# A four-layer graph network on one core: full-array products in the record scatter, and an accumulator added by an identity product

## The chip, the cores and the metric

The kernel runs on one core of one Trainium2 chip. A core has five engines that run beside each other: TensorE (matrix products; its weight loads are a row of their own in the profile, PEld), VectorE (DVE), ScalarE (ACT), GpSimd (POOL) and SyncE (SP, which here only issues transfers). The metric is the device time of one execution in microseconds (us). The kernel is one program; its stages follow each other with a barrier between them.

## The reference, cut to what matters

A graph of N = 3125 nodes with 256 features and E = 103125 edges (src, dst). Four layers follow each other, each on a normalised x:

```python
h = relu(layernorm(x)); x = x + L0(h, edges, edge_attr_18)     # attention, 16 heads, segments by src
h = relu(layernorm(x)); x = x + L1(h, edges, edge_attr_64, w)  # edge attention, 8 heads, by dst, and a feed-forward
h = relu(layernorm(x)); x = x + L2(h, edges, edge_type_8)      # relation sums, batch norm
h = relu(layernorm(x)); x = x + L3(h, edges)                   # attention, 4 heads, by dst
```

The attention of L1, which one part of the change touches, is, with `s` the scores of an edge per head:

```python
s   = (q[dst] * (k[src] + ef @ We + be)).sum(-1) * scale * edge_weight
ex  = exp(s - segment_max(s, dst)[dst])
out = segment_sum(ex / segment_sum(ex, dst)[dst] * v[src], dst) @ Wo + bo
```

## The kernel before, in words

**Sorting.** The edges are first put in order of their segment, once by src and once by dst. A node number is split into a high part (its block of BN = 126 nodes, NB = 25 blocks) and a low part (its place in the block). Edges come in tiles of 128, eight tiles (G) to a step, 101 steps. `scatter` (L497) runs once per order. Per step:
- VectorE (`position_ones`, L336) compares the keys with a row of numbers and writes one-hots: `hot_hi` (128 edges x 25 per tile) and `hot_lo` (128 x 128), in bf16.
- TensorE turns the high one-hots (L642) and ScalarE copies the result to `hot_hi_t` (25 x 128 per tile, f32, L564). L654 spreads the keys over rows, for the rank within a tile (VectorE, L608).
- A table of 25 x 128 counts says where the next edge of each node goes. L670 adds a pair of tiles to it in PSUM; ScalarE copies it to `table` (L577), two buffers in turn. L675 looks up: `hot_hi_t` of a tile is the stationary operand, the table the moving one, f32, contracting over the 25 high values. Each f32 product is two instructions. VectorE picks the low column (L616) and adds the rank: the position (L625).
- GpSimd writes each tile's records to DRAM with one indirect DMA (L545), eight per step, and waits for the positions, for the attributes that SP loads and for words that ScalarE copies (L588).

Beside the first scatter the high and low counts of the second order are summed (L717). Beside the second one, the q, k and v rows of the first layer are computed: once in four steps TensorE does one full-size f32 product (L845).

**The edge layer.** `edge_layer` (L956) runs for the kinds 0, 1 and 3, each 107 steps of eight tiles. The four engines work on different steps at once; `lagging` gives the step before (older), two before (oldest) and three before (gone). Per step, in kind 1:
- SP loads the records; GpSimd gathers 128 rows of k and v per tile with an indirect DMA (L1120) into one of four buffers, which is free once the sums of four steps ago are done.
- TensorE, in this order: the rest of the expansion of q to edges (L1190), the turned scores (L1204), the sums of the oldest step's first two pairs of tiles (L1230), more expansion, spread low keys (L1142), the turned exponentials (L1217, L1218), the sums of the last two pairs, and the preparation of the step after next.
- VectorE: the edge part is added to k (L1499, half a step at a time), multiplied with q (L1509), reduced to scores (L1532), scaled by the edge's weight (L1538); two scans find the maxima of the segments (L1444, L1448); the oldest step's v is weighed with the exponentials (L1476).
- ScalarE: the one-hots that place edges in rows (L1302, L1311, L1330, L1335), the exponentials (L1340), and `move_sums`, which copies each pair's sums from PSUM to `pair_sums` (L1357).
- A pair of tiles lies in one block of nodes. Its sums (128 x 272) are added to that block's slice of the accumulator `acc` by VectorE (`add_sums`, L1465), four adds per step, a step after the copy. The block's number is loaded to a register (`blocks_of`). The last two rows of `pair_sums` (segments that go on in the next tile) go to DRAM (L1360).

The order on each engine is the order of the calls in its `body`, and semaphores join them; nothing is reordered.

## Time and profile before

| | us |
|---|---|
| median of 3 runs | 8586.36 (8586.0 to 8587.62) |
| the profiled execution | 8571.41 |
| its span, first to last instruction | 8569.7 |
| TensorE busy | 6613.0 (77%) |
| VectorE busy | 5308.7 (62%) |
| GpSimd busy | 5221.6 (61%) |
| ScalarE busy | 3576.5 (42%) |
| mean granted TensorE clock | 0.784 of 2.4 GHz |

The busy shares are means over stages with different limits, so each stage is read by itself. The first scatter issues its DMAs from 285.0 to 1331.6 us, the second from 1359.6 to 2393.4; the layer of kind 0 follows, and that of kind 1 gathers from 4041.8 to 5413.8. Busy times of TensorE are modelled at their ends and overlap a little; for a group of products the distance from its start to the next group's start says more than the durations. Instructions that only issue or wait are not counted as busy. A granted clock of 0.50 is 1.2 GHz, 1.00 is 2.4 GHz.

### The profile page before, as it was taken

The page shows a single profiled execution, that of the slowest core. Times are in us where ns is not written, and L with a number is a line of the kernel's source. Part 1 is how long each engine was busy: PE and PEld are TensorE (multiplying, and loading weights), DVE is VectorE, ACT ScalarE, POOL GpSimd, SP SyncE. Part 2 cuts the span into 40 slices and gives each one's busy share as a digit, 9 for nine tenths or more (in the row PEclk, how much of TensorE's full clock was granted, in tenths as well). Part 3 has the DMA queues.
Part 4 walks back from the last instruction along what each step waited for, and adds up shares of the span by engine and source line. Part 5 has one row for each costly group of instructions (what it writes and reads, how often), then busy time and mean ns, then how long its engine had stood idle before and what let it go on. Part 6 is the DMA issues. An engine that isn't in the chain of part 4 may idle for free. (4 is left out here: it accounts for less than half of the span.)

```text
span 8569.7 us, 143502 instructions
## 1 busy us (share of the span) xinstructions
PE 6613.0 (77%) x33110; PEld 4732.5 (55%) x33111; DVE 5308.7 (62%) x15263; ACT 3576.5 (42%) x10766; POOL 5221.6 (61%) x5120
## 2 busy tenths in 40 slices
PE   7999998999979989974777777667855555667675
PEld 6777775666646666652555555455433344445454
DVE  6677776666657777774999999721122223455556
ACT  3322222333347666632666666223200000777772
POOL 0477776777767777721777777200277775677772
PEclk9655555555589999997999999879877777887887
DMA  7411111111145555532666666200344443444442
GB/s 219 136 17 16 17 17 26 33 33 34 33 106 140 138 136 138 140 61 96 184 175 175 176 178 175 85 11 33 132 108 108 108 108 80 107 110 109 109 108 47
DMA packets 1013468, 849.20 MB, mean 99 GB/s; under 512 B 751678, under 2 KB 841581, under 8 KB 1009339
## 3 DMA queue, kind: packets, MB, share of 16 engines
q0 software_dynamic: 257152, 645.64, 27.7%
q1 hardware_dynamic: 710069, 154.62, 9.1%
q10 hardware_dynamic: 45780, 44.08, 1.5%
q14 instruction: 341, 2.79, 0.1%
q8 instruction: 126, 2.06, 0.1%
HBM read 723.28 MB, written 120.67 MB: 98 GB/s over the span
## 5 line engine op out<-in xcount | busy, mean ns | idle before, releaser
L1120 POOL DMA_INDIRECT edges_kv<-kv,edges_rec x1712 | 1998.4, 1167 | 968.0 <-issue 511.0
L1230 PE MATMUL banks<-edges_kv,edges_hot 128*128 128x288 f32 (+2 forms) x5136 | 1563.8, 455 | 623.3 <-DVE edges_kv L1476 412.9
L1230 PEld LDWEIGHTS banks<-edges_kv,edges_hot 128*128 128x128 f32 x5136 | 1051.9, 215 | 1005.0 <-issue 563.6
L1631 POOL DMA_INDIRECT edges_rows<-rel,edges_rec x856 | 809.3, 945 | 965.2 <-DMA edges_rec<-by_dst_records 710.0
L545 POOL DMA_INDIRECT by_src_records<-sort_by_src_rec,sort_pos_i x808 | 773.9, 958 | 544.2 <-issue 533.2
L1120 POOL DMA_INDIRECT edges_kv<-feat,edges_rec x856 | 829.3, 969 | 270.4 <-issue 253.9
L675 PE MATMUL banks<-sort_table,sort_hot_hi_t 25*128 25x128 f32 x3232 | 952.1, 444 | 52.0 <-DVE sort_junk L616 47.2
L1647 PE MATMUL banks<-edges_rows,edges_hot 128*128 128x256 f32 x1712 | 625.8, 529 | 466.1 <-DMA edges_rows<-rel,edges_rec 449.2
L545 POOL DMA_INDIRECT by_dst_records<-sort_by_dst_rec,sort_pos_i x808 | 773.7, 958 | 288.0 <-issue 250.3
L1465 DVE TENSOR_TENSOR acc<-edges_pair_sums,acc 128x288 f32 (+2 forms) x1284 | 560.6, 437 | 487.0 <-DMA edges_kv<-feat,edges_rec 268.7
L675 PEld LDWEIGHTS banks<-sort_table,sort_hot_hi_t 25*128 25x128 f32 x3232 | 721.5, 307 | 221.2 <-issue 121.1
L1647 PEld LDWEIGHTS banks<-edges_rows,edges_hot 128*128 128x128 f32 x1712 | 428.0, 262 | 664.3 <-issue 404.0
L616 DVE SCALAR_TENSOR_TENSOR sort_junk<-banks,sort_hot_lo 128x128 bf16<-128x128 f32 x1616 | 435.3, 287 | 578.0 <-PE banks L675 537.5
L1330 ACT ACTIVATE edges_off<-columns,edges_column 128x128 bf16<-128x128 f32 x2568 | 784.6, 390 | 0.0
L1679 DVE TENSOR_TENSOR agg<-banks,agg 128x256 f32 x428 | 181.7, 424 | 768.8 <-PE banks L1647 768.8
L1302 ACT ACTIVATE edges_apart<-banks,minus_p 128x512 bf16<-128x512 f32 x642 | 429.3, 686 | 435.0 <-PE banks L1142 226.8
L608 DVE SCALAR_TENSOR_TENSOR sort_junk<-banks,sort_key_cur,sort_earlier 128x128 bf16<-128x128 f32 x1616 | 575.6, 411 | 6.0 <-PE banks L654 6.0
L1357 ACT COPY edges_pair_sums<-banks 128x288 f32<-128x288 f32 (+2 forms) x1284 | 460.7, 383 | 275.6 <-PE banks L1230 246.8
L1476 DVE TENSOR_TENSOR edges_kv<-edges_kv 128x1024 f32<-128x1024 f32 x428 | 518.8, 1212 | 0.0
L577 ACT COPY sort_table<-banks 25x128 f32<-25x128 f32 x808 | 204.8, 254 | 728.2 <-PE banks L670 728.2
L564 ACT COPY sort_hot_hi_t<-banks 25x512 f32<-25x512 f32 x404 | 231.9, 574 | 647.2 <-PE banks L642 647.2
L1190 PE MATMUL banks<-x,edges_hot_t 128*128 x1712 | 476.5, 403 | 3.4 <-DVE edges_kv L1509 3.4
(372 smaller groups left out, 12506.6 us busy)
## 6 DMA issues: line engine op xcount, KB each, us to landing
edges_kv<-kv,edges_rec POOLq DMA_INDIRECT x1712
sort_feat<-in_edge_attr_dram SPq DMA_DIRECT2D x100, 256.0 KB, 3.6
rel<-tables_stage SPq DMA_DIRECT2D x25, 1008.0 KB
by_dst_records<-by_dst_blank ACTq DMA_DIRECT2D x1, 17120.0 KB, 54.2
edges_rec<-by_dst_records SPq DMA_DIRECT2D x107, 160.0 KB
edges_rows<-rel,edges_rec POOLq DMA_INDIRECT x856
edges_kv<-feat,edges_rec POOLq DMA_INDIRECT x856
by_src_records<-sort_by_src_rec,sort_pos_i POOLq DMA_INDIRECT x808, 2.1
```

Of the source, the lines that this page charges most:

```text
L545: pool.indirect_dma_start(O.rec, bass.IndirectOffsetOnAxis(ap=pos_i[:, u, c:c + 1], axis=0), rec[:, u, c, :], None).then_inc(scattered[u], 16)
L608: last = dve.scalar_tensor_tensor(out=junk[:, 0, c, 0:P + mates].rearrange("p (t e) -> p t e", e=P), in0=ps[:, 4 + h, end - P - mates:end] ...
L675: pe.matmul(ps[:, 2 + c % 2, 0:P], hot_hi_t[:, u, c, :], table[:, d % 2, :], start=True, stop=True).then_inc(looked_up, 1)
L1120: pool.indirect_dma_start(kv[:, r, c, 0:koff + DIM], None, tab, bass.IndirectOffsetOnAxis(ap=reci[:, r, c, idx:idx + 1], axis=0)).then_inc ...
L1190: last = pe.matmul(out[:, c, 2 * P - QW:2 * P], hot_t[:, b % 2, 2 * m + c, :], rows, start=(kind == 1), stop=(kind == 1 or c == 1), skip_g ...
L1230: last = pe.matmul(ps[:, 6 + m % 2, 0:OW], hot[:, b % 2, c, :], kv[:, b % BUFS, c, koff:koff + OW], start=(c % 2 == 0), stop=(c % 2 == 1))
L1330: last = act.activation(off[:, c, :], C.columns[:, c % 2, :], ACT.Abs, bias=column[:, b % 2, c:c + 1], scale=-1.0)
L1357: act.copy(pair_sums[:, m, :], ps[:, 6 + m % 2, 0:OW]).then_inc(sums_copied, 1)
L1465: dve.tensor_tensor(rows, pair_sums[:, m, :], rows, ALU.add).then_inc(added, 1)
L1476: dve.tensor_tensor(v4, v4, bc(exps, dh), ALU.mult).then_inc(msg_done, 1)
L1631: pool.indirect_dma_start(rows[:, b, c, :], None, tab, bass.IndirectOffsetOnAxis(ap=reci[:, b, c, idx:idx + 1], axis=0)).then_inc(gathered ...
L1647: last = pe.matmul(ps[:, m, 0:DIM], hot[:, b, c, :], rows[:, b, c, :], start=(c % 2 == 0), stop=(c % 2 == 1))
```

## The change

In `scatter`, the tiles that feed three products are made 128 high or wide, with zeros in what was not there; the zeros are written once, by GpSimd, at the start. The products L642, L670 and L675 run over all of it. In the edge layer of kind 1, VectorE's adds go; TensorE adds the accumulator's block to the pair's sums in PSUM by a product with the identity, and ScalarE copies the sum back to the accumulator, and the 32 rows from 96 on to `pair_sums`. Each such product waits until the accumulator of the pair before it has been stored. ScalarE's third pair moves into `one_hot`, between the two passes of the one-hots.

```diff
-        hot_hi = ph.sbuf("hot_hi", [P, 2, G, NB], BF16)
+        hot_hi = ph.sbuf("hot_hi", [P, 2, G, P], BF16)
-        hot_hi_t = ph.sbuf("hot_hi_t", [NB, 2, G, P])
+        hot_hi_t = ph.sbuf("hot_hi_t", [P, 2, G, P])
-        table = ph.sbuf("table", [NB, 2, P])
+        table = ph.sbuf("table", [P, 2, P])
...
+                pool.memset(table[:], 0.0).then_inc(filled, 1)
+                pool.memset(hot_hi_t[:], 0.0).then_inc(filled, 1)
+                pool.memset(hot_hi[:], 0.0).then_inc(filled, 1)
...
-                            last = pe.matmul(ps[0:NB, 0, P * c:P * c + P], hot_hi[:, b % 2, 4 * h + c, :], C.ident_b[:],
+                            last = pe.matmul(ps[:, 0, P * c:P * c + P], hot_hi[:, b % 2, 4 * h + c, :], C.ident_b[:],
...
-                                last = pe.matmul(ps[0:NB, TABLE, 0:P], hot_hi[:, u, c, :], hot_lo[:, u, c, :],
+                                last = pe.matmul(ps[:, TABLE, 0:P], hot_hi[:, u, c, :], hot_lo[:, u, c, :],
...
                         for c in (2 * m, 2 * m + 1):
                             last = pe.matmul(ps[:, 6 + m % 2, 0:OW], hot[:, b % 2, c, :], kv[:, b % BUFS, c, koff:koff + OW],
-                                             start=(c % 2 == 0), stop=(c % 2 == 1))
-                        last.then_inc(summed, 1)
+                                             start=(c % 2 == 0), stop=(kind != 1 and c % 2 == 1))
+                        if kind != 1:
+                            last.then_inc(summed, 1)
+
+                def with_past(j, b, m):
+
+                    n = at(j, b)
+                    block = blocks_of(pe, O, j, b, UNROLL)[m]
+                    if not (first_steps(j, b, 1) and m == 0):
+                        pe.wait_ge(acc_kept, n(PAIRS, m))
+                    pe.matmul(ps[:, 6 + m % 2, 0:OW], C.ident[0:BN, :],
+                              acc[0:BN, bass.ds(block, 1), :].rearrange("p o w -> p (o w)"), start=False, stop=True).then_inc(summed, 1)
...
                     if oldest:
                         sums(*oldest, 0)
+                        if kind == 1:
+                            with_past(*oldest, 0)
                     if inside:
                         expand(j, b, (3,))
+                    if oldest and kind == 1:
+                        with_past(*oldest, 1)
...
                     if oldest:
                         sums(*oldest, 1)
+                        if kind == 1:
+                            with_past(*oldest, 2)
                     if ahead:
                         expand(*ahead, (1,))
                     if beyond:
                         front(*beyond)
+                    if oldest and kind == 1:
+                        with_past(*oldest, 3)
...
-                def move_sums(j, b, h):
+                def move_sums(j, b, pairs):
...
+                    blocks = blocks_of(act, O, j, b, UNROLL) if kind == 1 else None
+                    for m in pairs:
                         act.wait_ge(summed, n(PAIRS, m + 1))
+                        if kind == 1:
+                            act.copy(acc[:, bass.ds(blocks[m], 1), :].rearrange("p o w -> p (o w)"), ps[:, 6 + m % 2, 0:OW]
+                                     ).then_inc(acc_kept, 1)
+                            act.copy(pair_sums[ENDS:P, m, :], ps[ENDS:P, 6 + m % 2, 0:OW]).then_inc(sums_copied, 1)
+                            continue
...
+                    if between:
+                        move_sums(*between, (2,))
...
                     older, oldest, gone = (lagging(j, b, lag) for lag in (1, 2, 3))
+                    if kind == 1:
+                        gone = None
```

`ENDS` is 96. Not shown: the slices `0:NB` where the 25 rows or columns are written, and `move_sums` being called for the pairs (0, 1), (2) and (3) instead of two halves.

## Rows read from the trace of the kernel before

**Rows 1.** Windows, first and second scatter: stretch, length, busy (count) by engine, granted clock, DMA, GB/s.
```profile
285.10:1331.70 1046.60, 973.00 (x5582) 729.90 (x5581) 769.70 (x3699) 272.37 (x1192) 772.93 (x808) 0.50 0.16 28
1359.70:2393.40 1033.70, 939.44 (x4918) 647.05 (x4918) 668.68 (x3660) 312.51 (x1464) 772.68 (x808) 0.54 0.16 33
```

**Rows 2.** Line L545: count, ns min/median/max, first and last start.
```profile
L545 POOL DMA_INDIRECT by_src_records<-sort_by_src_rec,sort_pos_i x808: 952/958/1177, 285.0 to 1331.6; - x162
L545 POOL DMA_INDIRECT by_dst_records<-sort_by_dst_rec,sort_pos_i x808: 952/958/973, 1359.6 to 2393.4; - x162
```

**Rows 3.** Order of time, first scatter: start, us, engine, line, [idle before].
```profile
1001.71 0.96 POOL L545 DMA_INDIRECT by_src_records<-sort_by_src_rec,sort_pos_i  x1 [0.30 <-issue]
...
1002.16 0.12 PEld L670 LDWEIGHTS banks<-sort_hot_lo,sort_hot_hi 128*25 128x25 bf16 x2 [0.23 <-issue]
...
1006.65 0.11 PEld L654 LDWEIGHTS banks<-sort_ident_hi,sort_halves 128*128 128x128 bf16 x1 [0.20 <-issue]
```

**Rows 4.** Line L1532: count, ns min/median/max, first and last start.
```profile
L1532 DVE TENSOR_REDUCE edges_score_raw<-edges_kv x107: 2268/2270/2286, 4058.9 to 5422.2; 128x64 f32<-128x2048 f32 x107
```

**Rows 5.** Window of the edge layer of kind 1.
```profile
4058.97:5422.25 1363.28, 1030.06 (x4733) 761.82 (x4731) 1269.79 (x2110) 853.78 (x2318) 1051.76 (x844) 0.94 0.64 176
```

**Rows 6.** Order of time in kind 1: VectorE, and one GpSimd issue.
```profile
4804.78 2.27 DVE L1532 TENSOR_REDUCE edges_score_raw<-edges_kv 128x64 f32<-128x2048 f32 x1
...
4807.46 1.21 DVE L1499 TENSOR_TENSOR edges_kv<-edges_kv,edges_rec 128x1024 f32<-128x1024 f32 x1
4808.59 0.43 DVE L1465 TENSOR_TENSOR acc<-edges_pair_sums,acc 128x272 f32 x1
4808.95 1.27 DVE L1509 TENSOR_TENSOR edges_kv<-banks,edges_kv 128x512 f32<-128x512 f32 x2
4810.15 1.21 DVE L1476 TENSOR_TENSOR edges_kv<-edges_kv 128x1024 f32<-128x1024 f32 x1
4811.28 0.43 DVE L1465 TENSOR_TENSOR acc<-edges_pair_sums,acc 128x272 f32 x1
...
4812.93 1.21 DVE L1499 TENSOR_TENSOR edges_kv<-edges_kv,edges_rec 128x1024 f32<-128x1024 f32 x1
...
4816.75 2.27 DVE L1532 TENSOR_REDUCE edges_score_raw<-edges_kv 128x64 f32<-128x2048 f32 x1
...
4810.15 2.38 POOL L1120 DMA_INDIRECT edges_kv<-kv,edges_rec  x1 [0.31 <-issue]
```

**Rows 7.** By line, same stretch: count, busy us, mean ns, idle before and its releasers.
```profile
L1120 POOL DMA_INDIRECT edges_kv<-kv,edges_rec x844 | 1052.0, 1246 | 304.4 <-issue 242.8 <-PE banks L1230 61.6
...
L1499 DVE TENSOR_TENSOR edges_kv<-edges_kv,edges_rec 128x1024 f32<-128x1024 f32 x212 | 257.5, 1215 | 59.7 <-DMA edges_kv<-kv,edges_rec 38.9 <-issue 20.6
...
L1465 DVE TENSOR_TENSOR acc<-edges_pair_sums,acc 128x272 f32 x415 | 177.7, 428 | 0.0
L1357 ACT COPY edges_pair_sums<-banks 128x272 f32<-128x272 f32 x418 | 148.4, 380 | 64.2 <-PE banks L1230 56.1
```

**Rows 8.** Order of time, second scatter, TensorE.
```profile
1534.35 1.22 PE L675 MATMUL banks<-sort_table,sort_hot_hi_t 25*128 25x128 f32 x4
...
1536.86 3.72 PE L845 MATMUL banks<-sort_qkv_w,sort_cur_t 128*128 128x512 f32 x4
...
1542.45 0.71 PE L675 MATMUL banks<-sort_table,sort_hot_hi_t 25*128 25x128 f32 x4
```

**Rows 9.** Order of time, the start of the kernel.
```profile
13.26 0.64 POOL L274 MEMSET sort_by_dst_rec<- 128x640 f32 x1
...
54.92 1.76 SPq L407 DMA_DIRECT2D sort_feat<-in_edge_attr_dram  x4
```

**Rows 10.** Order of time in kind 1: TensorE, and ScalarE.
```profile
4811.45 2.07 PE L1230 MATMUL banks<-edges_kv,edges_hot 128*128 128x272 f32 x8 [1.82 <-issue]
4813.36 1.03 PE L1190 MATMUL banks<-x,edges_hot_t 128*128 x4
...
4804.40 2.45 ACT L1330 ACTIVATE edges_off<-columns,edges_column 128x128 bf16<-128x128 f32 x8
```

More of the change, by code:

```diff
@@ L552, in _ @@
                 def _(act):
-                    act.copy(table[:, 0, :], starts[:]).then_inc(table_ready, 1)
+                    act.copy(table[0:NB, 0, :], starts[:]).then_inc(table_ready, 1)
                     beside.scalar_start(act)
@@ L563, in turn @@
                         act.wait_ge(turned, at(j, b)(2, h + 1))
-                        act.copy(hot_hi_t[:, b % 2, 4 * h:4 * h + 4, :], ps[0:NB, 0, :].rearrange("k (c e) -> k c e", c=4)
+                        act.copy(hot_hi_t[0:NB, b % 2, 4 * h:4 * h + 4, :], ps[0:NB, 0, :].rearrange("k (c e) -> k c e", c=4)
                                  ).then_inc(turned_copied, 1)
@@ L576, in body @@
                             act.wait_ge(looked_up, n(G, 2 * d))
-                            act.copy(table[:, (d + 1) % 2, :], ps[0:NB, TABLE, 0:P]).then_inc(table_ready, 1)
+                            act.copy(table[0:NB, (d + 1) % 2, :], ps[0:NB, TABLE, 0:P]).then_inc(table_ready, 1)
                             if ahead and d == 0:
@@ L631, in _ @@
                 def _(pe):
-                    pe.matmul(ps[0:NB, TABLE, 0:P], C.zeros_b[:, 0:NB], C.zeros_b[:], start=True, stop=False, skip_group_check=True)
+                    pe.matmul(ps[:, TABLE, 0:P], C.zeros_b[:], C.zeros_b[:], start=True, stop=False, skip_group_check=True)
                     pe.matmul(ps[0:NB, TABLE, 0:P], C.ident[0:NB, 0:NB], starts[:], start=False, stop=False, skip_group_check=True)
@@ L972, in edge_layer @@
     UNROLL = 12
+    ENDS = 96
     ROUNDS = -(-STEPS // UNROLL)
@@ L1081, in edge_layer @@
         added = ph.sem("added")
+        acc_kept = ph.sem("acc_kept")
         dve_set = ph.sem("dve_set")
@@ L1324, in front, with one_hot @@
                     last.then_inc(front_copied, 1)
-                def one_hot(j, b):
+                def one_hot(j, b, between=None):
                     n = at(j, b)
@@ L1346, in tails @@
                              ps[:, 0, 2 * P:2 * P + 2 * HG].rearrange("p (i c h) -> p i c h", i=2, c=G)).then_inc(tail_copied, 1)
-                def move_sums(j, b, h):
+                def move_sums(j, b, pairs):
                     n = at(j, b)
-                    if h == 0:
+                    if 0 in pairs:
                         act.wait_ge(ends_out, n(16, 0))
-                    for m in (2 * h, 2 * h + 1):
+                    blocks = blocks_of(act, O, j, b, UNROLL) if kind == 1 else None
+                    for m in pairs:
                         act.wait_ge(summed, n(PAIRS, m + 1))
+                        if kind == 1:
[3 more added lines that the diff above has]
+                            continue
                         if not first_steps(j, b, 1):
@@ L1357, in move_sums @@
                         act.copy(pair_sums[:, m, :], ps[:, 6 + m % 2, 0:OW]).then_inc(sums_copied, 1)
-                    if h == 1:
+                    if PAIRS - 1 in pairs:
                         act.wait_ge(sums_copied, n(PAIRS, PAIRS))
@@ L1385, in body @@
                     if oldest:
-                        move_sums(*oldest, 0)
+                        move_sums(*oldest, (0, 1))
                     if ahead and kind < 3:
@@ L1394, in body @@
                     if older:
-                        one_hot(*older)
+                        one_hot(*older, oldest if kind == 1 else None)
+                    elif oldest and kind == 1:
+                        move_sums(*oldest, (2,))
                     if older and kind == 3:
@@ L1398, in body @@
                     if oldest:
-                        move_sums(*oldest, 1)
+                        move_sums(*oldest, (3,) if kind == 1 else (2, 3))
                 steps(act, body)
```

2 lines of the change are left out of this document (1 added, 1 removed).

## The prediction

> **What bounds the kernel now.** I read the busy shares by slice first and kept the two stretches that the change touches: the scatter of sorted records (L497 to L683, run twice) and the edge layer of kind 1 (L956 to L1578). Then the windows of each, then the work grouped by line, then the order of work in single steps.
>
> The scatters look bound by TensorE: it is busy 973.00 of 1046.60 us and 939.44 of 1033.70 us, at a granted clock of 0.50 and 0.54 of 2.4 GHz [rows 1]. They are not. GpSimd issues 808 indirect DMAs in each; from first to last start it needs (1331.6 - 285.0) / 807 = 1.297 us per DMA in the first and (2393.4 - 1359.6) / 807 = 1.281 in the second [rows 2], and a DMA with nothing to wait for costs 0.96 + 0.30 = 1.26 us [rows 3]. So 98% of each scatter is GpSimd's own issue time, and TensorE sits just under it.
>
> The edge layer has 107 steps. The last reduction starts at 5422.2, the first at 4058.9 [rows 4]: 1363.3 / 106 = 12.86 us per step. VectorE is busy 1269.79 of 1363.28 us [rows 5], and a step without a disturbance takes 4816.75 - 4804.78 = 11.97 us [rows 6], in which VectorE never rests. GpSimd: (1052.0 busy + 242.8 issue gap) / 844 x 8 = 12.27 us per step, and 61.6 / 844 x 8 = 0.58 us more in which it waits for L1230 to free a buffer [rows 7]: 12.85 together, the whole step. VectorE in turn waited 59.7 us before L1499, mostly for gathers [rows 7]. So two engines share the bound: GpSimd's issue (12.27), VectorE (11.97), and 0.59 us lost because neither is steady.
>
> **The change, part by part: the scatter.** Removed: nothing. L642, L670 and L675 keep their number and their moving columns; the high one-hot is 128 columns wide as a stationary operand where it was 25, and L675 contracts over 128 rows where it was 25. Each first weight load took 0.12 us at 25 columns and 0.11 us at 128 [rows 3], so at the same clock the cost is nil; bounds from the 0.01 us either way, on 6 first loads a step and 202 steps: -12 to +12 us of TensorE, which lies beside GpSimd.
>
> Can the clock change? In the second scatter the one full-array f32 product, L845, runs 3.72 us; L675 before it costs 1.22 us a group and after it 0.71 us [rows 8]. The same L675 with its 25 rows ran 93% of the first scatter [rows 1] and never left 1.2 GHz. So full-array work is what preceded the rise, and the change makes three more products full-array. I expect a higher clock in both scatters.
>
> The Trainium skill, "TensorE: Matmul & The Clock Gate", section "Part 1: The HAM clock gate", says that a busy TensorE releases the throttle. The trace speaks against it as it stands: 93% busy and throttled. By the page's rule, which knows only busy or idle, the change would lift nothing.
>
> What is a higher clock worth? Little. The first scatter loses 0.016 us per DMA against the second, 807 x 0.016 = 13 us, and both together lose 807 x (0.037 + 0.021) = 47 us against the bare 1.26. Not all of that is TensorE's: the second scatter has its clock raised in part already, and both wait for records and code. I take 10 us, nearest to the 13 by which the two differ. Bounds: 0 and 47. Next to be late is GpSimd itself, which nothing here makes faster.
>
> Three more memsets on GpSimd (256 f32, 2048 f32 and 2048 bf16 per partition): 640 f32 took 0.64 us, so about 4.4 us behind the memsets at 13.3 us. This block ends with SP's loads; SP's first DMA of the next one starts at 54.92 [rows 9]; they are hidden, and would cost their 4.4 us without that cover.
>
> **The edge layer of kind 1.** Removed: four L1465 adds per step on VectorE. Each fills 4808.95 - 4808.59 = 0.36 us of its line (0.428 by its own duration, less the overlap) [rows 6, 7]: about 4 x 0.35 = 1.40 us. One of them covers the time between the reduction and the product that waits for it; I give back 0.1. VectorE: 11.97 - 1.40 + 0.1 = 10.7 us.
>
> Added on TensorE: four f32 products per step, 126 rows, 272 moving columns, each two instructions. The eight instructions of L1230 take 4813.36 - 4811.45 = 1.91 us [rows 10], so one product 0.48 us and four 1.9. TensorE was busy (1030.06 / 1363.28) x 12.86 = 9.7 us a step [rows 5] and becomes 11.6.
>
> Added on ScalarE: four more copies, by the 0.380 us of L1357 [rows 7] 1.5 us on an engine that is busy 853.78 of 1363.28, or 8.1 us a step [rows 5]: 9.6, no bound.
>
> Moved, and the new waits: product m waits until ScalarE has stored the accumulator of product m-1. Behind the waiting product stand L1190 and the transposes, for which VectorE waits. Of the four waits, m=0 is long fulfilled. Between m=0 and m=1 lie the expansion L1190 (1.03 us), longer than one copy of 0.38: covered. m=2 is old. m=3 waits for a copy that ScalarE makes after its eight L1330 (2.45 us) [rows 10]; behind it are the next expansion and the transpose of the scores. The first product alone costs VectorE something: L1230 starts at 4811.45, L1190 ends at 4813.36 + 1.03 = 4814.39 [rows 10], and becomes 4814.87. VectorE wants that bank after the scan block (4812.93 - 4811.28 - 0.35 = 1.30), L1499 (4808.59 - 4807.46 = 1.13) and half of the two L1509 (0.60): 4811.28 + 3.03 = 4814.31 [rows 6]. It waits 0.56: 11.25 us. TensorE's own 11.6 includes overlaps and slow-clock time, so I take 11.5 for the ring of VectorE, TensorE and ScalarE; its bounds are 10.7 (every wait covered) and 11.6 + 4 x (0.38 + 0.1) = 13.5 (no copy covered).
>
> GpSimd. Its mean issue is 1.246 us in this stage against 0.95 undisturbed. The one that starts at 4810.15 takes 2.38 us and ends at 4812.53, 0.90 us after the slot of L1465 (4811.28 + 0.35 = 4811.63) [rows 6]. So an issue that begins under L1476 and L1465 starts anew when they end; under the reduction L1532 none does. The stretching costs 12.27 - 8 x 1.25 = 2.3 us per step. The ops that do it fill 2 x 1.13 (L1499), 2 x 1.13 (L1476) and 1.40 (L1465) us: by time L1465's share is 24%; by the square of each unbroken stretch (three of 1.49, one of 1.13 and one of 0.34 become four of 1.13) it is 37%. I take 30%, 0.7 us: GpSimd 11.6 us per step; bounds 0 (another op merely takes the place) and 0.85.
>
> The Trainium skill, "SBUF — State Buffer", section "SBUF: two separate sides", says that a VectorE instruction with two SBUF inputs shuts out a GpSimd operation that reads SBUF until it ends. L1465, L1476 and L1499 have two SBUF inputs, L1509 and L1532 have not, and the trace agrees with the 2.38 us.
>
> The sum. The slower of 11.5 and 11.6, and the same 0.59 lost to unsteadiness: 12.2 us. (12.86 - 12.2) x 106 = 70 us. The profiled execution takes 8571.41 us, 8569.7 of it the span; 8571.4 - 10 - 70 = 8491. The median of the runs, 8586.36, lies 15.0 above the profiled time: **8506 us**.
>
> **The rivals.**
> - Steadier than before: with 1.27 us less VectorE work the engines stop disturbing each other, and a step falls to about 11.5. 1.36 x 106 = 144 us, with the scatter 154: 8432. For it: the gathers that came late did so behind long issues. Against it: after a late gather TensorE drops to 1.2 GHz (mean 0.94 here [rows 5]), and it now has 1.9 us more to catch up with.
> - GpSimd isn't relieved: its 12.27 stays, with half of the 0.59: 12.56, 32 us, 10 from the scatter: 8544; with none of either 8586. For it: issues fall by turns on one op or another.
> - Slower: the ring closes through ScalarE. In the in-order queue of TensorE the product m=3 waits behind L1330, the next step's scores wait behind it, and VectorE's scan behind them. At the 13.5 bound a step costs 0.64 more: +68, less 10: 8644. It decides from the point where the ring exceeds 12.86, that is where 1.4 us of the copies and of the register loads ahead of each product lie open. For it: every step at 1.2 GHz doubles TensorE's 1.9. Against it: two of the four waits are covered by a microsecond.
> - The widening doesn't lift the clock: then the scatter gives 0: 8516.
> - The scatters are TensorE-bound after all: at full clock some 40% of the 973 + 939 us would go, 760 us. The 1.26 of [rows 3] excludes nearly all of it.
>
> **How the numbers follow.** Forecast 0.45; same with the clock not lifted 0.15; steadier 0.14; GpSimd unrelieved 0.12; slower 0.11; TensorE-bound scatters 0.03. Likeliest case alone: 8465 to 8550. Range for 8 in 10: 8430 to 8590, from the steadier case to no change at all. This kernel's runs tell apart 0.2%, 17 us. Faster: 0.45 + 0.15 + 0.14 + 0.03, plus half of the unrelieved case, less 0.04 for shortfalls within 17 us: 0.79. Same 0.09, slower 0.12.
>
> **What would show it.** Right: clock near 1 in the scatters with L675 near 0.7 us a group, yet 1.26 to 1.28 us per DMA of L545; L1532 starting every 11.3 to 11.6 us when undisturbed and 12.2 on average; L1120 in this layer near 1.16 us; L1465 gone there. Wrong: scatters shorter by over 47 us; L1120 still at 1.24; VectorE waiting over 1 us per step before L1444 or L1509 for TensorE.

## The result, and the profile after

The changed kernel takes 8542.28 us, the median of 5 runs (8530.89 to 8547.64); the kernel before took 8586.0 (8579.67 to 8587.62) beside it. The ratio is 0.995, with a 95% interval of 0.9936 to 0.9965: faster, by 44 us. The forecast was 8506 in a range of 8430 to 8590. So direction and range held, but the gain is about half of the 80 us forecast.

The profiled execution took 8530.89 us, its span 8529.2, against 8571.41 and 8569.7. First the windows of the two scatters (columns as in [rows 1]) and the scattering line (as in [rows 2]) of the changed kernel:

```profile
280.00:1313.90 1033.90, 698.13 (x5577) 607.05 (x5577) 758.60 (x3699) 272.55 (x1190) 772.90 (x808) 0.75 0.17 29
1339.20:2368.00 1028.80, 691.42 (x4918) 577.36 (x4918) 653.16 (x3662) 313.10 (x1464) 772.70 (x807) 0.75 0.16 33
```

```profile
L548 POOL DMA_INDIRECT by_src_records<-sort_by_src_rec,sort_pos_i x808: 954/958/1177, 279.9 to 1313.9; - x162
L548 POOL DMA_INDIRECT by_dst_records<-sort_by_dst_rec,sort_pos_i x808: 952/958/975, 1339.2 to 2368.0; - x162
```

The granted clock rose from 0.50 and 0.54 to 0.75, and TensorE's busy time fell by 275 and 248 us. Yet a scatter needs 1034.0 / 807 = 1.281 and 1028.8 / 807 = 1.275 us per DMA, against 1.297 and 1.281: 12.6 and 5.0 us won.

Then the edge layer of kind 1: its window, its last reduction, and the work by line, to be read against [rows 4, 5, 7]:

```profile
4033.20:5363.00 1329.80, 1202.11 (x5568) 880.42 (x5566) 1164.29 (x1695) 1016.58 (x2729) 902.82 (x843) 0.98 0.66 181
```

```profile
L1565 DVE TENSOR_REDUCE edges_score_raw<-edges_kv x107: 2272/2279/2289, 4033.2 to 5362.9; 128x64 f32<-128x2048 f32 x107
```

```profile
L1125 POOL DMA_INDIRECT edges_kv<-kv,edges_rec x843 | 903.1, 1071 | 417.0 <-issue 272.1 <-PE banks L1246 144.9
...
L1532 DVE TENSOR_TENSOR edges_kv<-edges_kv,edges_rec 128x1024 f32<-128x1024 f32 x212 | 260.0, 1227 | 66.3 <-DMA edges_kv<-kv,edges_rec 43.0 <-issue 22.6
...
L1542 DVE TENSOR_TENSOR edges_kv<-banks,edges_kv 128x512 f32<-128x512 f32 x424 | 276.9, 687 | 33.5 <-PE banks L1195 11.0
...
L1477 DVE TENSOR_TENSOR_SCAN edges_run_max<-edges_pen,banks 64x128 f32<-64x128 f32 x106 | 43.5, 410 | 60.9 <-PE banks L1209 60.5
...
L1246 PE MATMUL banks<-acc,ident 126*128 x836 | 281.0, 417 | 48.6 <-ACT acc L1382 38.3 <-issue 5.1
...
L1382 ACT COPY acc<-banks 128x272 f32 x418 | 158.9, 380 | 170.4 <-PE banks L1246 162.7 <-DMA ends<-edges_pair_sums 4.0 <-issue 0.6
```

From first to last reduction 1329.7 us, 12.54 a step, against 1363.3 and 12.86. VectorE is 105 us less busy. A gather issue takes 1.071 us in place of 1.246 [rows 7]. But GpSimd now waits 144.9 us for L1246, where it waited 61.6 for L1230, and VectorE waits 60.5 us for L1209 before its scan, where it waited for nothing. The order of time shows where that wait and VectorE's new one come from, in one step without a disturbance (TensorE, ScalarE, GpSimd, VectorE in turn):

```profile
4362.81 2.00 PE L1235 MATMUL banks<-edges_kv,edges_hot 128*128 128x272 f32 x8
4364.64 0.62 PE L1246 MATMUL banks<-acc,ident 126*128 x2
...
4367.08 0.72 PE L1246 MATMUL banks<-acc,ident 126*128 x2 [0.37 <-ACT acc L1382]
4367.97 1.12 PE L1195 MATMUL banks<-x,edges_hot_t 128*128 x4 [0.17 <-issue]
4368.93 0.27 PE L1209 MATMUL banks<-ident,edges_score 128*64 128x128 f32 x1
...
4364.00 2.44 ACT L1353 ACTIVATE edges_off<-columns,edges_column 128x128 bf16<-128x128 f32 x8
4366.35 0.36 ACT L1382 COPY acc<-banks 128x272 f32 x1
...
4363.51 0.94 POOL L1125 DMA_INDIRECT edges_kv<-kv,edges_rec  x1 [0.30 <-issue]
...
4368.61 0.94 POOL L1125 DMA_INDIRECT edges_kv<-kv,edges_rec  x1 [1.66 <-PE banks L1246]
...
4371.17 1.41 POOL L1125 DMA_INDIRECT edges_kv<-kv,edges_rec  x1 [0.30 <-issue]
...
4362.30 2.28 DVE L1565 TENSOR_REDUCE edges_score_raw<-edges_kv 128x64 f32<-128x2048 f32 x1
...
4364.75 1.25 DVE L1532 TENSOR_TENSOR edges_kv<-edges_kv,edges_rec 128x1024 f32<-128x1024 f32 x1
4366.13 1.29 DVE L1542 TENSOR_TENSOR edges_kv<-banks,edges_kv 128x512 f32<-128x512 f32 x2
...
4369.24 0.41 DVE L1477 TENSOR_TENSOR_SCAN edges_run_max<-edges_pen,banks 64x128 f32<-64x128 f32 x1 [0.69 <-PE banks L1209]
...
4370.55 1.21 DVE L1532 TENSOR_TENSOR edges_kv<-edges_kv,edges_rec 128x1024 f32<-128x1024 f32 x1
...
4374.22 2.28 DVE L1565 TENSOR_REDUCE edges_score_raw<-edges_kv 128x64 f32<-128x2048 f32 x1
```

Read it from ScalarE: its copy of the third pair stands behind eight one-hot activations and ends at 4366.71. The fourth product (4367.08) waits for it; the expansion L1195 and the turned scores L1209 stand behind that product, and VectorE waits 0.69 us for these. GpSimd's next buffer is given free by the same product: it counts up `summed`, for which the gathers wait. The sums of that pair (L1235) ended at 4364.81, the product ends at 4367.80: the buffer comes free 3.0 us later than without it. The step takes 4374.22 - 4362.30 = 11.92 us, as before the change (11.97, [rows 6]).

The same rows show what stretches an issue. The one at 4363.51 runs under the reduction L1565, which reads one operand from SBUF, and takes 0.94 us. The one at 4371.17 starts under L1532, which reads two, and ends at 4372.58, 0.82 us after L1532 has (4371.76). In the whole layer each of the 158 issues of over 1.2 us ends 0.80 to 0.84 us after a VectorE instruction with two SBUF operands (L1532 or L1509), and no issue that lies wholly under L1565 takes over 0.96. Before the change 245 issues took over 1.2 us, all of them so, the additions L1465 included.

The gain lies in the disturbed steps. From one start of L1565 to the next the median step is 11.96 us and was 11.97. Before, 16 of the 106 steps took over 15 us, now 6, each at a jump back of the loop, whose body holds 12 steps. And TensorE's granted clock in the layer is 0.98, where it was 0.94 [rows 5]: it stood at 0.50 for a part of 33 steps before and of 8 after, and what these steps took beyond 11.97 us each adds up to 89 us before and 39 after. The products fill TensorE, which rested 1.82 us ahead of L1230 in a step before [rows 10]. Whether the steadier clock makes the steps steady or the other way round, no run separates.

The balance by spans: to the end of the second scatter 25.4 us less (12.6 and 5.0 in the scatters, 5.1 because the first one begins at 279.9 and not 285.0, 2.7 between them), to the first reduction 0.3, in the layer 33.6. Behind the layer 10.3 are given back: the next stage's first instruction stands at 5391.50, 28.6 us behind the last reduction, and stood 5440.54 - 5422.2 = 18.3 behind it.

```profile
5440.54 0.33 POOL L1744 MEMSET combine_conts<- 128x273 f32 x1 [25.76 <-POOLq L78]
```

```profile
5382.05 0.39 ACT L1382 COPY acc<-banks 128x272 f32 x1 [2.08 <-PE banks L1246]
...
5382.77 0.72 PE L1246 MATMUL banks<-acc,ident 126*128 x2 [1.00 <-ACT acc L1382]
...
5391.50 0.33 POOL L1779 MEMSET combine_conts<- 128x273 f32 x1 [38.78 <-POOLq L78]
```

The first fence is of before, the second of after. In the drain of the last steps nothing covers a copy, and product and copy run strictly in turn. The remaining 8.5 us come after that, in code that isn't changed: the layer of kind 3 ran 1092.2 us from first to last L1520, against 1081.2. It took 1091.0 to 1095.7 in three later kernels that keep the change in the edge layer (copy_early, late_unroll24, past_late), and 1085.2 to 1089.2 in the five of the next section, which leave the edge layers as they were. The two groups don't overlap, so not all of this is scatter between profiled runs; its cause stays open. 25.4 + 0.3 + 33.6 - 10.3 - 8.5 = 40.5, the difference of the spans.

### The profile page after: what moved, and what is told of

Its sections match the earlier page's. It is cut to its first block and busy times, and to the rows that moved or that the text cites. A ratio compares the mean times of both kernels' runs of the same rounds, so it can differ in the third digit from the quotient of the medians.

```text
span 8529.2 us, 146143 instructions
## 1 busy us (share of the span) xinstructions
PE 6270.4 (74%) x33966; PEld 4667.0 (55%) x33967; DVE 5172.4 (61%) x14835; ACT 3745.6 (44%) x11195; POOL 5081.3 (60%) x5123
## 5 line engine op out<-in xcount | busy, mean ns | idle before, releaser
L1125 POOL DMA_INDIRECT edges_kv<-kv,edges_rec x1712 | 1853.6, 1083 | 1073.2 <-issue 534.5
L1235 PE MATMUL banks<-edges_kv,edges_hot 128*128 128x288 f32 (+2 forms) x5136 | 1515.2, 444 | 303.7 <-DVE edges_kv L1509 259.1
L1235 PEld LDWEIGHTS banks<-edges_kv,edges_hot 128*128 128x128 f32 x5136 | 1040.5, 212 | 627.2 <-issue 301.3
L678 PE MATMUL banks<-sort_table,sort_hot_hi_t 128*128 128x128 f32 x3232 | 739.3, 367 | 264.1 <-DVE sort_junk L619 264.1
L678 PEld LDWEIGHTS banks<-sort_table,sort_hot_hi_t 128*128 128x128 f32 x3232 | 593.7, 258 | 301.5 <-DVE sort_junk L619 297.1
L1498 DVE TENSOR_TENSOR acc<-edges_pair_sums,acc 128x288 f32 (+1 forms) x856 | 377.7, 441 | 476.5 <-DMA edges_kv<-feat,edges_rec 241.8
L619 DVE SCALAR_TENSOR_TENSOR sort_junk<-banks,sort_hot_lo 128x128 bf16<-128x128 f32 x1616 | 412.9, 288 | 359.1 <-PE banks L678 345.3
L1509 DVE TENSOR_TENSOR edges_kv<-edges_kv 128x1024 f32<-128x1024 f32 x428 | 520.6, 1217 | 3.5 <-ACT edges_kv L1370 3.5
L1195 PE MATMUL banks<-x,edges_hot_t 128*128 x1712 | 469.2, 397 | 59.1 <-issue 44.0
L1542 DVE TENSOR_TENSOR edges_kv<-banks,edges_kv 128x256 f32<-128x256 f32 (+1 forms) x856 | 441.1, 553 | 46.2 <-PE banks L1195 14.7
```

Source lines behind the costliest of these rows:

```text
L678: pe.matmul(ps[:, 2 + c % 2, 0:P], hot_hi_t[:, u, c, :], table[:, d % 2, :], start=True, stop=True).then_inc(looked_up, 1)
L1125: pool.indirect_dma_start(kv[:, r, c, 0:koff + DIM], None, tab, bass.IndirectOffsetOnAxis(ap=reci[:, r, c, idx:idx + 1], axis=0)).then_inc ...
L1195: last = pe.matmul(out[:, c, 2 * P - QW:2 * P], hot_t[:, b % 2, 2 * m + c, :], rows, start=(kind == 1), stop=(kind == 1 or c == 1), skip_g ...
L1235: last = pe.matmul(ps[:, 6 + m % 2, 0:OW], hot[:, b % 2, c, :], kv[:, b % BUFS, c, koff:koff + OW], start=(c % 2 == 0), stop=(kind != 1 an ...
L1509: dve.tensor_tensor(v4, v4, bc(exps, dh), ALU.mult).then_inc(msg_done, 1)
L1542: dve.tensor_tensor(k2, by, k2, ALU.mult).then_inc(edges_used, 1)
```

## Experiments on the scatter

All of these ran on two chips where the kernel before takes 8577 and 8582 us. scatter_wide is the kernel before with the change's first part alone. lookup_tall has only the tall operands of the lookup, onehot_wide only the wide one-hots:

```
lookup_tall:  -hot_hi_t = ph.sbuf("hot_hi_t", [NB, 2, G, P])        +[P, 2, G, P]     (table likewise)
onehot_wide:  -hot_hi = ph.sbuf("hot_hi", [P, 2, G, NB], BF16)      +[P, 2, G, P]
              -pe.matmul(ps[0:NB, TABLE, 0:P], hot_hi[:, u, c, :], ...   +pe.matmul(ps[:, TABLE, 0:P], ...
```

> The kernel before with the scatter's part of the change alone. Theory (two parts that add up): the whole sort stage falls from 2407 to about 2383 us as in the changed kernel, everything else stays, and the kernel is 20 to 28 us faster than before, ratio 0.997. Rival (the parts interact, or the scatter's gain is the layer's): the sort stage falls by less than 10 us.

> Of the scatter's part only the height: the looked-up table and the turned one-hots have 128 rows (L675 contracts over 128), the high one-hots stay 25 columns wide. Theory (L675, the longest work of TensorE here, sets the clock): the granted clock in the scatters rises nearly as in the changed kernel (there 0.75 to 0.8 from 0.50) and the sort stage falls by 20 us or more. Rival (the width of the one-hots is as needed): the clock stays under 0.65 and the stage falls by less than 10 us.

> Of the scatter's part only the width: the high one-hots are 128 columns wide (L642 and L670), L675 contracts over 25 rows as before. Theory: the clock stays at 0.50 to 0.55 and the sort stage within 5 us of before, 2407 us. Rival (the width is what counts): the clock rises over 0.65.

Measured: scatter_wide 8559.44 us, ratio 0.9978 (0.9968 to 0.9988); lookup_tall 8557.58, 0.9981 (0.9972 to 0.9991); onehot_wide 8564.18, 0.9988 (0.9978 to 0.9997). That is 17, 19 and 13 us, scatter_wide a little less than its 20 to 28. The second scatter's last DMA starts at 2370.2 in scatter_wide, 23.2 us earlier than before. The windows of the two scatters in lookup_tall, and then in onehot_wide:

```profile
282.60:1316.90 1034.30, 728.30 (x5577) 559.07 (x5577) 762.13 (x3699) 272.92 (x1190) 772.88 (x808) 0.78 0.17 29
1342.90:2371.60 1028.70, 755.04 (x4918) 541.38 (x4918) 658.64 (x3660) 312.46 (x1464) 772.60 (x808) 0.75 0.16 33
```

```profile
284.70:1319.40 1034.70, 962.68 (x5582) 742.33 (x5581) 769.80 (x3699) 273.71 (x1192) 773.10 (x808) 0.50 0.17 29
1346.90:2375.90 1029.00, 886.47 (x4918) 664.35 (x4918) 663.08 (x3662) 314.44 (x1465) 772.78 (x807) 0.56 0.16 33
```

The height alone lifts the clock; the width alone leaves it at 0.50 in the first scatter, where TensorE is 93% busy. And still both have the scatters of 1034 and 1029 us. So the clock rises as forecast, by the lookup, but it is not what the gain needs: 10 us less of TensorE work at 1.2 GHz (962.68 for 973.00) went with the same gain. The expectation for onehot_wide missed this: its last DMA starts 17.5 us earlier than before (2375.9), not within 5.

To see TensorE without GpSimd in its way, half_narrow leaves out every other indirect DMA in the kernel before (half of the sorted records are never written), and half_wide does the same in scatter_wide:

```
-for c in range(G):            +for c in range(0, G, 2):
     pool.indirect_dma_start(O.rec, ...)        (and half the count in each wait on `scattered`)
```

> The kernel before with every second of GpSimd's scatter DMAs left out, so half of the sorted records stay blank. Theory (GpSimd's issue covers a TensorE that is nearly as long): without GpSimd's bound the scatters shrink only a little, to TensorE's own pace at 1.2 GHz: 9.3 to 10.0 us per step where it was 10.36 and 10.24, each scatter 940 to 1010 us. Rival (TensorE is far from the bound): a step falls to 8.5 us or less, to what VectorE's 7.6 us of work allow.

> The two scatters with every other indirect DMA left out (half of the sorted records are never written), and with the tall lookup and the wide one-hots. It is half_narrow with the widening added. half_narrow's first scatter took 1037.0 us at 1.2 GHz, a step of 10.31 us, with GpSimd's need halved to 5.05 us; so TensorE alone needed about as much as GpSimd's 10.10. Theory: the widening lifts the clock and TensorE's need falls to about 7 us (busy 701.65 us in 101 steps of scatter_wide); VectorE's 7.6 us of work is next, so a step takes 7.8 to 8.6 us and each scatter 790 to 870 us; the clock then has a worth of some 170 us per scatter that GpSimd's issue hides. Rival: the chain from one step's table to the next (TensorE, ScalarE, VectorE in turn) sets about 9.5 to 10.1 us whatever the clock, and each scatter stays over 950 us.

One run each, on two chips: half_narrow 8562.53 us, half_wide 8240.92. The windows of half_narrow, then of half_wide:

```profile
281.70:1318.70 1037.00, 973.01 (x5582) 729.94 (x5581) 769.62 (x3699) 272.35 (x1191) 385.84 (x404) 0.50 0.14 24
1350.30:2374.10 1023.80, 939.47 (x4918) 647.18 (x4918) 668.47 (x3660) 312.79 (x1464) 385.66 (x404) 0.54 0.13 26
```

```profile
283.50:1179.00 895.50, 627.49 (x5577) 540.17 (x5577) 757.16 (x3699) 272.31 (x1190) 387.17 (x404) 0.83 0.16 28
1207.70:2037.40 829.70, 610.46 (x4918) 510.54 (x4918) 653.13 (x3660) 314.12 (x1464) 386.92 (x404) 0.83 0.16 31
```

With GpSimd's need halved the narrow scatters are about as long as before, 1037.0 and 1023.8: TensorE at 1.2 GHz needed a little more than GpSimd, about 10.3 us a step against 8 x 1.26 = 10.1. Both scatters lie above the expected 940 to 1010. Step by step (from one step's first L545 to the next one's) half_narrow's first scatter repeats 10.23, 10.39, 10.31 and 10.50 us. The kernel before has 39 steps of that pace among the 100 of its first scatter; most others take GpSimd's 10.10. The changed kernel and onehot_wide have one. Besides, every 14th step took about 12.0 us and takes 11.5 in these two. So the two engines were tied, and a little less of TensorE's work was all that the scatter could use. With the wide operands the same two scatters take 895.5 and 829.7, 336 us less. That is what the higher clock is worth where GpSimd doesn't bind; with all of the DMAs its issues leave 18. The first scatter missed the expected 790 to 870 by 25 us, the second is within.

## Experiments on the edge layer

Four kernels ran on another chip, on which the kernel before takes 10320.68 us; there its scatters and other stages that nobody changed are longer too. They are to be read by their ratios and among themselves: neither the kernel before nor the changed one has a trace from that chip.

no_adds is the kernel before with the four additions left out and no product in their place, so that nothing is accumulated (ScalarE's wait for the additions goes too):

```
+if kind == 1:
+    gone = None
+    last_add = None
```

> The kernel before with VectorE's four adds per step left out in the layer of kind 1 and nothing in their place: the accumulator of that layer stays zero. Theory (the ring): the changed kernel got all the relief of VectorE and GpSimd, and lost it again on TensorE's waiting products; then this kernel, without products, runs its undisturbed step at about 10.7 us (11.97 less 1.40, plus 0.1), with GpSimd's mean issue near the 1.071 us of the changed kernel, and the layer takes 1230 to 1280 us where it took 1363 (first to last reduction). Rival (GpSimd bound): with the adds gone GpSimd still needs over 1.2 us per issue and the step stays at 12 us or more: 1300 us or over.

Measured: 10415.27 us, ratio 1.0094 (1.0061 to 1.0127), a miss: slower, with less work. Its lines show why it says little: the scan L1444 waited 305.9 us for an event that the profile gives no source for (its line in the kernel before waited 12.3 us in all three layers, for named work), TensorE rests, and the clock is 0.84. What holds it there stays open; waits without a source stand in its first scatter too, where nothing was changed (L616, 368.8 us), and in none of the kernel before on the first chip. The mean issue is 1.079 us, near the expected 1.071, but beside a VectorE that waits.

filler_sbuf and filler_one put VectorE work back into the changed kernel in the places of the additions, four a step. In one it has two SBUF inputs, in the other one:

```
filler_sbuf: +dve.tensor_tensor(spare[:, 2], spare[:, 0], spare[:, 1], ALU.add)
filler_one:  +dve.tensor_reduce(spare[:, 2, 0:8], spare[:, 0].rearrange("p (a b) -> p a b", a=8), AX_X, ALU.add)
```

> The changed kernel with four more VectorE instructions per step in kind 1, at the places of the former adds: a tensor_tensor of two operands in SBUF, 256 columns, 0.35 us each. Theory (adds stretch GpSimd's issues): GpSimd's mean issue goes back from 1.071 towards the 1.246 us of before, to about 1.2, and the layer to 1370 to 1420 us. Rival (GpSimd was relieved by the slower, steadier rhythm of the engines): its mean issue stays at 1.10 or less, and the layer grows only as VectorE does.

> The same with four reductions of one SBUF operand, 256 columns, of about the same length in place of the tensor_tensor. Theory (two SBUF operands are what stretches the issues): GpSimd's mean issue stays near 1.07 to 1.10 us, and the layer is 20 to 60 us shorter than with the tensor_tensor, 1340 to 1370 us. Rival (any VectorE work does it): both fillers give the same issue time within 0.02 us and the same layer time within 10 us.

past_free keeps the four products, but they read a tile of zeros and wait for no copy (the accumulation is left out); ScalarE's copy waits for its own predecessor in their place:

```
-pe.wait_ge(acc_kept, n(PAIRS, m))
 pe.matmul(ps[:, 6 + m % 2, 0:OW], C.ident[0:BN, :],
-          acc[0:BN, bass.ds(block, 1), :]...        +nothing[0:BN, :]
```

> The changed kernel with the four products of kind 1 kept, but their moving operand is a tile of zeros and they wait for no accumulator: the sums of a block are not carried from pair to pair. Theory (the ring): the waits for ScalarE's copies, above all the fourth pair's behind the eight one-hot activations, close the ring at 11.9 us per step; without them the undisturbed step falls to 11.2 to 11.5 us and the layer to about 1270 us from 1330. Rival (TensorE's bare work): the four products themselves fill TensorE (it is busy 1202 of 1330 us), and the step stays at 11.8 to 11.9 us, the layer within 10 us of 1330.

Measured: filler_sbuf 10256.66 us, 0.9922 (0.9893 to 0.9951); filler_one 10282.93, 0.9955 (0.9938 to 0.9972); past_free 10198.34, 0.9874 (0.9847 to 0.9901). GpSimd's line in the layer, of filler_sbuf, of filler_one and of past_free:

```profile
L1126 POOL DMA_INDIRECT edges_kv<-kv,edges_rec x837 | 946.6, 1131 | 561.8 <-issue 315.6 <-PE banks L1247 238.6 <-remote 7.6
```

```profile
L1126 POOL DMA_INDIRECT edges_kv<-kv,edges_rec x836 | 928.3, 1110 | 562.7 <-issue 332.5 <-PE banks L1247 228.2 <-remote 2.0
```

```profile
L1126 POOL DMA_INDIRECT edges_kv<-kv,edges_rec x839 | 973.4, 1160 | 446.4 <-issue 292.3 <-PE banks L1245 142.4 <-remote 11.7
```

The mean issues differ by 1.131 - 1.110 = 0.021 us, 0.17 us a step, and the profiled layers, 1515.7 and 1498.8 us, by 0.16 us a step. But the medians stand the other way round, 10256.66 and 10282.93, and the profiled run of filler_sbuf is its slowest, 10299.57. So no difference in time is shown, and both expectations are missed (an issue of about 1.2 us, and one of 1.07 to 1.10 with a layer 20 to 60 us shorter). The single issues tell more. With the one-input fillers 165 issues take over 1.2 us; each ends 0.80 to 0.84 us after one of the layer's own two-operand instructions, and none so after a filler. With the two-input fillers 31 of 186 end so after a filler. The Trainium skill, "SBUF — State Buffer", section "SBUF: two separate sides", has a two-input instruction of VectorE shut GpSimd out. The traces agree, issue by issue. Without the waits (past_free) the layer takes 1429.8 us, 69 us less than with one-input fillers, with a longer mean issue (1.160) and shorter waits: the mean depends also on which instructions the issues happen to start under. Its layer is far from the 1270 us expected and from the rival's 1330, and the changed kernel didn't run on this chip, so past_free doesn't decide between the two.

The last three ran on a chip where the kernel before takes 8582.25 us; the changed kernel's traces are of another one. The layer of kind 0, which they share, takes 1298.9 and 1297.2 us in the first two and 1290.2 in the changed kernel, so a difference of some 9 us means nothing there. past_late moves the fourth product of a step one body later:

```
 if older:
     turn_scores(*older)
+gone = lagging(j, b, 3)
+if gone and kind == 1:
+    with_past(*gone, 3)
...
-if oldest and kind == 1:
-    with_past(*oldest, 3)
```

> The changed kernel with one thing moved: the fourth accumulator product of a step is issued one body later on TensorE, behind the turn of the scores, so that the expansion of targets and the turned scores no longer queue behind ScalarE's third copy. Theory (the ring through that wait sets the undisturbed step of 11.9 us): VectorE's wait of 0.7 us for the turned scores goes, the undisturbed step falls to 11.2 to 11.5 us, first to last reduction of the kind-1 layer from 1329.7 to 1275 to 1300 us, the whole 30 to 55 us faster than the changed kernel. Rival: the same 0.48 us of product only stands ahead of another transfer (the sums of the next pair), and the step stays at 11.8 to 12.0, the layer within 10 us of 1329.7. Second rival: the longer hold on the buffer that the gathered features are read from makes GpSimd wait; then its waits for the sums grow over 200 us.

Measured: 8605.87 us, 1.0027 (1.0014 to 1.004), the layer 5430.1 - 4045.0 = 1385.1 us: 55 slower than the changed kernel, where 30 to 55 less were expected. Two reductions of one step, and the work by line:

```profile
4166.40 2.28 DVE L1566 TENSOR_REDUCE edges_score_raw<-edges_kv 128x64 f32<-128x2048 f32 x1
...
4176.14 0.69 DVE L1543 TENSOR_TENSOR edges_kv<-banks,edges_kv 128x512 f32<-128x512 f32 x1 [0.46 <-PE banks L1195]
...
4177.88 2.28 DVE L1566 TENSOR_REDUCE edges_score_raw<-edges_kv 128x64 f32<-128x2048 f32 x1
```

```profile
L1125 POOL DMA_INDIRECT edges_kv<-kv,edges_rec x844 | 954.2, 1131 | 421.2 <-issue 267.2 <-PE banks L1246 154.1
...
L1533 DVE TENSOR_TENSOR edges_kv<-edges_kv,edges_rec 128x1024 f32<-128x1024 f32 x212 | 260.1, 1227 | 138.8 <-DMA edges_kv<-kv,edges_rec 115.6 <-issue 23.0
...
L1543 DVE TENSOR_TENSOR edges_kv<-banks,edges_kv 128x512 f32<-128x512 f32 x425 | 280.8, 688 | 75.9 <-PE banks L1195 53.4
...
L1478 DVE TENSOR_TENSOR_SCAN edges_run_max<-edges_pen,banks 64x128 f32<-64x128 f32 x106 | 43.0, 406 | 0.1
```

The first half of the theory is shown: the wait for the turned scores is gone (60.9 to 0.1 us), and a step can take 11.48 us. The second half fell. VectorE gives back what it won and more, in two places: it waits for late gathers, 43.0 to 115.6 us, and for the expansion L1195 ahead of L1543, 11.0 to 53.4, which came in time when VectorE was 0.69 us late. Less the 60.8 won, that is 54 of the 55 us. The issues go from 1.071 to 1.131 us, 0.48 us over 8, and the step grew by 13.07 - 12.54 = 0.53. More of them start under a two-operand instruction: 205 take over 1.2 us, where 158 did. The second rival, a wait of GpSimd over 200 us, didn't come (154.1). So VectorE's 0.69 us of rest cost little in the mean: without it the gathers and the expansion are late. That GpSimd's round (issues, and the wait for the buffer) is what then binds is argued from this, and not shown; past_late also frees the buffer later still.

copy_early has ScalarE copy the third pair after four of the eight one-hot activations:

```
 for c in range(G):
+    if between and c == G // 2:
+        move_sums(*between, (2,))
     last = act.activation(off[:, c, :], ...)
```

> The changed kernel with ScalarE's copy of the third pair's sums issued after four of its eight one-hot activations and not behind all eight; nothing else. Theory: the wait of the fourth product on TensorE for that copy (0.37 us in the step at 4367.08) goes, the expansion and the turned scores come 0.3 to 0.4 us earlier, the undisturbed step falls to 11.4 to 11.7, the layer to 1290 to 1315 us. Rival: the sums of the third pair aren't ready that early; ScalarE then waits with four activations behind it, the one-hots of the next expansion come late, and the layer is no shorter or up to 30 us longer.

Measured: 8612.7 us, 1.0042 (1.0026 to 1.0059), the layer 5437.2 - 4040.6 = 1396.6 us. In its layer:

```profile
L1125 POOL DMA_INDIRECT edges_kv<-kv,edges_rec x843 | 977.6, 1160 | 409.5 <-issue 272.4 <-PE banks L1246 137.1
...
L1542 DVE TENSOR_TENSOR edges_kv<-banks,edges_kv 128x512 f32<-128x512 f32 x424 | 283.2, 689 | 86.7 <-PE banks L1195 63.7
L1246 PE MATMUL banks<-acc,ident 126*128 x836 | 281.8, 418 | 94.5 <-ACT acc L1382 93.6 <-issue 0.2
...
L1235 PE MATMUL banks<-edges_kv,edges_hot 128*128 128x272 f32 x1672 | 444.5, 410 | 54.9 <-ACT edges_hot L1360 48.1 <-issue 3.5 <-DVE edges_kv L1509 3.3
```

The rival's mechanism came: TensorE waits 48.1 us for the one-hots. The theory's didn't: TensorE waits 93.6 us for ScalarE's copies, where it waited 38.3. The layer is 67 us longer, beyond the rival's 30. VectorE waits 63.7 us for L1195, and again the issues are longer, by 0.089 us, 0.71 a step, beside the step's 0.63.

late_unroll24 is past_late with longer loop bodies:

```
-UNROLL = 12        +UNROLL = 24
```

> past_late with 24 steps per turn of the loop in the edge layers in place of 12, so half as many jumps back. In the changed kernel the step at each jump takes 18 to 20 us against 12, about 7 us lost, some six or seven times in each of the three edge layers. Theory: the loss belongs to the jump: half of the jumps go, 3 layers x 3 or 4 x 6 to 7 us, 55 to 85 us less than past_late. Rival: the loss belongs to the amount of code that has to be brought in, the same however it is cut; then it is within 15 us of past_late.

Measured: 8538.03 us, 0.9948 (0.9934 to 0.9961), 68 us less than past_late and within the measurement of the changed kernel. The layer takes 5363.8 - 4010.7 = 1353.1 us (32 less), the one of kind 0 takes 1269.7 from first to last reduction where past_late takes 1298.9, and the one of kind 3 is unchanged, against the expectation of a gain in all three. In this layer the long steps at four of the six jumps are gone with the jumps, and the two that are left stay long. So here the loss sits at the jump back. In the changed kernel, one of six in this layer:

```profile
4614.13 2.28 DVE L1565 TENSOR_REDUCE edges_score_raw<-edges_kv 128x64 f32<-128x2048 f32 x1
...
4620.52 1.22 DVE L1532 TENSOR_TENSOR edges_kv<-edges_kv,edges_rec 128x1024 f32<-128x1024 f32 x1 [3.85 <-issue]
...
4624.72 2.07 PE L1195 MATMUL banks<-x,edges_hot_t 128*128 x4 [5.46 <-issue]
...
4633.35 2.28 DVE L1565 TENSOR_REDUCE edges_score_raw<-edges_kv 128x64 f32<-128x2048 f32 x1
```

This step takes 19.22 us, 7.3 more than an undisturbed one. VectorE has 3.85 us of it with nothing to wait for and TensorE 5.46; then TensorE's granted clock is 0.50, and four L1195 take 2.07 us where they took 1.12 [4367.97 above]. Twenty-four steps a body on the changed kernel itself was not tried.

## Why the prediction was right, and where its sizes were off

- **The scatter.** The clock rose, the bound stayed with GpSimd's 1.26 us, and 1.281 and 1.275 us per DMA lie at the upper edge of the 1.26 to 1.28 named. The term was 10 us and measured 17.6, 25 with the blocks around. Of the 25, 5.1 are only an earlier start. It was undersized because I read TensorE as sitting "just under" GpSimd; half_narrow shows that it was tied or just over. GpSimd's own issue time was 97% of the first scatter (807 x 1.26 of 1046.6), not 98. And the 0.12 us at 25 columns [rows 3] are of two weight loads: onehot_wide's are 12.4 us busier than before in the first scatter (742.33), which the bound of 12 just misses; it cost nothing. The rival of TensorE-bound scatters is refuted as a gain of 760 us and was right about the tie. The Trainium skill's "TensorE: Matmul & The Clock Gate", section "Part 1: The HAM clock gate", knows only a busy TensorE or an idle one. onehot_wide, 93% busy and at 0.50, beside lookup_tall, 70% busy and at 0.78, speaks against it here.
- **VectorE, 10.7 us.** The undisturbed step of 11.92 with 0.69 of rest gives 11.23. Of the 1.40 us that the additions filled, only 11.97 - 11.23 = 0.74 came back: L1542 now starts 4366.13 - 4364.75 = 1.38 us behind L1532, where the addition started 1.13 behind its predecessor and ended 0.36 later [rows 6]: 0.11 saved for 0.36 taken away. It had stood in the time in which the next operation waits for a result anyway. I gave back 0.1 for one such place.
- **The ring of VectorE, TensorE and ScalarE.** Forecast 11.5, measured 11.23 + 0.69 = 11.92 in an undisturbed step: 0.4 us a step, 45 us of the layer, more than the 36 by which the layer missed its 70. That the waits are so near (0.56 and 0.69) is luck. I took the 0.56 from the first product, which makes the expansion late for L1509. That wait fell from 33.5 us in the layer to 11.0 (L1542 for L1195). The 0.69 comes from the fourth product, through ScalarE's third copy, and VectorE waits before its scan: the mechanism that I had only in the slower rival. My wait is hidden behind it: in past_late, where it is gone, L1543 waits 0.46 us for L1195 in the undisturbed step.
- **GpSimd, 11.6 us.** Relief forecast 0.7, measured larger: (903.1 + 272.1) / 843 x 8 = 11.15, down 1.12 from 12.27. The mechanism is the one forecast, an issue that ends after the two-operand instruction it started under; which issues meet one depends on the rhythm, and neither the share by time nor the one by squares has that.
- **What I overlooked.** I listed who waits behind the product on TensorE, and not who waits for the count that it now carries. `summed` moved from L1230 to the product, so GpSimd's buffer is free only after ScalarE's copy. Its wait grew from 0.58 to 144.9 / 843 x 8 = 1.38 us a step. 11.15 + 1.38 = 12.53, the whole step; but issues, gaps and waits of an engine always add up to the step, as 12.27 + 0.58 did in the prediction, and this doesn't make it the bound. In the undisturbed step GpSimd waits 1.66 of 11.92 us, so it has room there. How much the later buffer costs is open: no run gave the gathers back their count at L1235.
- **The 0.59 us of unsteadiness, kept.** The mean lies 12.54 - 11.92 = 0.62 above the undisturbed step; about 0.4 of it (6 x 7.3 / 106) are the jumps back. Before, 0.89 lay above it. So the undisturbed step is unchanged, and the 33.6 us came from fewer disturbed ones: that is the steadier rival's mechanism, at a quarter of its size. The sum had its 70 us from a shorter undisturbed step, so within the layer it is right in sign for another reason. My argument against the rival, that TensorE has more to catch up with when its clock has dropped, came out the other way: the clock dropped in 8 steps, where it had in 33.
- **The drain.** 10.3 us that no term had, and 8.5 us behind it that stay unexplained.
- **The slower rival.** The wait through ScalarE is real, but at 11.9 the ring stays under 12.86, the point from which it would have decided.

## What to carry to other kernels

Where a completion count moves to a later instruction, price everyone who waits for that count, above all those who only wait for a buffer to be free. Where two engines lie within 3% of each other, as in both stages here, relief of one gave little, and a wait removed in one place came back in another. Look at disturbed steps apart from undisturbed ones: the mean can move while the median stays. Work between two dependent operations is worth less than its duration when it goes (0.11 us for 0.36 here).

## What the runs showed of the hardware

- The granted clock of the first scatter was 0.78 with a 128-row lookup and 25-column one-hots (lookup_tall), and 0.50 with a 25-row lookup and 128-column one-hots (onehot_wide).
- GpSimd's issue of one indirect DMA took 0.958 us in the scatters; in this layer 1.071 in the mean (1.246 before), 0.94 to 0.96 under an instruction of VectorE with one SBUF operand. One of over 1.2 us ended 0.80 to 0.84 us after an instruction with two (245 before, 158 after the change).
- The step at a jump back to the start of a loop body took 19.22 us where others take 11.92; in it TensorE stood 5.46 us and VectorE 3.85 with nothing to wait for.
- Chips differ: the kernel before took 8586 us on one and 10320.68 on another.
